# Tokens of v and k by DMA transposes, and the factor of v moved into the decays: a gated linear attention layer on eight cores

## Chip, cores, metric

One Trainium2 chip, eight cores, one program. The metric is the device time of the slowest core, in microseconds (us). Four cores (even numbers) take the first five tiles of a sequence, four (odd numbers) the last three after they have rebuilt the state of the first five.

## What is computed

x has shape (4, 4096, 1024). Cut to what matters here:

```python
h = layernorm(x)
q, k, v = split(silu(causal_conv4(h @ W_qkv.T)))      # 16 heads of 64
z = h @ W_z.T; beta = sigmoid(h @ W_b.T)
g = -exp(A_log) * softplus(h @ W_a.T + dt_bias)
q = l2norm(q) * 64**-0.5; k = l2norm(k)
S_t = S_{t-1} * exp(g_t) + k_t (v_t * beta_t)^T;  o_t = q_t S_t
x = x + (rmsnorm(o) * silu(z)) @ W_out.T
x = x + complex_linear(layernorm(x))                  # 1024 x 1024 in all
```

## The kernel before

The state is advanced in chunks of 128 tokens, four to a tile of 512. With A the running sum of g inside a chunk, a chunk's output is v times the masked product exp(A_t - A_s) (k_s . q_t), plus the old state read by q exp(A_t), and the state is multiplied by the chunk's whole decay and gets k exp(A_end - A_s) times v. beta and the norm of k are factors for each token and head. Before the change their product (beta over the norm) multiplies v, so it is in both uses of v.

Channels lie on partitions after projection and convolution (tile `post`). The two products that sum over tokens need v and k with tokens on partitions. `tvk(g)` does that: 16 transposes of 128x128 on TensorE (8 for v, L731; 8 for k, L735) into the two banks of `pA`, and two multiplications on VectorE that read `pA` and write `vtok` (L741, factor of v) and `ktil` (L746, factor of k). The factors come from `gates_a` to `gates_e`, once for a tile.

The work is software pipelined by hand. The main loop has a tile index t, running one behind the streamed tile u = t + 1, and a step s for each chunk. A step projects and convolves part of tile u, advances the chunk g = 4t + s, finishes the output projection of chunk n - 1 and the last linear layer of chunk n - 2. Each engine runs its instructions in the order in which the loop writes them. `fe` are projections (`proj`, L504, evacuated at L528 on ScalarE and L531 on VectorE), `fc` convolutions (L551) with SiLU (L557), `fz` projections of z. Odd cores run tiles 0 to 4 without outputs (four projections and four convolutions to a step, "state only" steps) and tiles 5 to 7 in full ("full" steps); even cores run five tiles in full. The last tile's four chunks run after the stream has ended, in a loop of their own (the drain).

SyncE (SP) issues nearly all DMAs from one ordered queue: the weights (`w_issue`, five buffers), the convolution's diagonals (`d_issue`, six buffers), rows of x, the stores, and the DMA transposes of the two layernorms (`lnxT` at L140, called from `ln1_norm`, and `ln2T`, from `ln2_norm`). GpSimd (POOL) issues the small loads and stores, masks the decays (L774), squares q (L809), adds the bias (L967) and decays the state (L859). `decay(n, 0)` uses the PSUM pair `pB`, `decay(n, 1)` the pair `pA`, and waits until `tvk` has been read out of it.

## Time and profile before

| | |
|---|---|
| three runs | 884.14 us median (883.65 to 891.31) |
| the profiled execution | 885.31 us |
| span of its slowest core (core 1) | 883.5 us |
| spans of all cores | 871.5 to 883.5 us |
| TensorE busy (core 1) | 680.0 us, 77% |
| VectorE, ScalarE, GpSimd busy | 447.9, 338.4, 192.5 us |
| DMA | 129.58 MB, mean 147 GB/s |

The span runs from the first to the last instruction of a core. The profiled execution took 1.8 us more than the span of its slowest core, and 1.2 us more than the median. The share of busy time is a mean over stages that have different limits, so it has to be read by stage.

### The profile page before, as it was taken

The page shows a single profiled execution, that of the slowest core. Times are in us where ns is not written, and L with a number is a line of the kernel's source. Part 1 is how long each engine was busy: PE and PEld are TensorE (multiplying, and loading weights), DVE is VectorE, ACT ScalarE, POOL GpSimd, SP SyncE. Part 2 cuts the span into 40 slices and gives each one's busy share as a digit, 9 for nine tenths or more (in the row PEclk, how much of TensorE's full clock was granted, in tenths as well). Part 3 has the DMA queues.
Part 4 walks back from the last instruction along what each step waited for, and adds up shares of the span by engine and source line. Part 5 has one row for each costly group of instructions (what it writes and reads, how often), then busy time and mean ns, then how long its engine had stood idle before and what let it go on. Part 6 is the DMA issues. An engine that isn't in the chain of part 4 may idle for free.

```text
span 883.5 us, 14594 instructions; the slowest of 8 cores (871.5 to 883.5 us)
## 1 busy us (share of the span) xinstructions
PE 680.0 (77%) x4872; PEld 317.5 (36%) x4872; DVE 447.9 (51%) x712; ACT 338.4 (38%) x579; POOL 192.5 (22%) x231
## 2 busy tenths in 40 slices
PE   0675569999996998988729997989799997744563
PEld 0322234444443444444204443434344443322221
DVE  2633436677675565445105457734355653557432
ACT  0143426556654464544204653413444433111100
POOL 2020000000001001012113305233142351644310
PEclk9987979999998899999859998989999998767788
DMA  6699458766669566569675556384563474033321
GB/s 150 153 204 194 131 143 214 191 159 190 156 189 222 162 158 193 154 149 172 147 193 167 157 152 164 96 167 118 148 182 93 135 163 102 26 84 86 84 83 36
DMA packets 109618, 129.58 MB, mean 147 GB/s; under 512 B 51990, under 2 KB 72732, under 8 KB 109408
## 3 DMA queue, kind: packets, MB, share of 16 engines
q1 hardware_dynamic: 98832, 106.73, 44.2%
q0 software_dynamic: 10704, 21.83, 14.0%
q8 instruction: 43, 0.70, 0.3%
q14 instruction: 39, 0.32, 0.1%
HBM read 111.39 MB, written 18.27 MB: 147 GB/s over the span
## 4 chain that ended last, share of the span: by engine, by line
PE 47%; DMA 17%; DVE 11%; issue 11%; ACT 9%; SPq 3%; POOL 2%; DVEq 1%; ACTq 0%; POOLq 0%
PE pRG L504 24%; PE pRG L551 6%; DMA dscr<-s_d 5%; PE pRG L934 3%; DMA s_rb<-rscr 3%; ACT s_post L557 3%; PE pB L934 3%; PE pA L976 3%; DMA s_lnxT<-s_lnx 2%; SPq L135 2%; DMA wscr<-s_w 2%; ACT L557 2%; PE pA L731 1%; DMA s_w<-wcat 1%; DMA rscr<-s_r 1%
## 5 line engine op out<-in xcount | busy, mean ns | idle before, releaser
L504 PE MATMUL pRG<-s_lnxT,s_w 128*128 128x512 bf16 x1408 | 341.3, 396 | 51.2 <-DVE s_pre L531 23.6
L504 PEld LDWEIGHTS pRG<-s_lnxT,s_w 128*128 128x128 bf16 x1408 | 136.6, 101 | 221.5 <-issue 82.8
L551 PE MATMUL pRG<-s_pre,s_d 128*128 128x512 bf16 x608 | 149.0, 385 | 10.5 <-ACT s_post L557 7.1
L557 ACT ACTIVATE s_post<-pRG 128x512 bf16<-128x512 f32 x152 | 86.0, 592 | 32.4 <-PE pRG L551 32.1
L528 ACT CAST s_pre<-pRG 128x512 bf16<-128x512 f32 x70 | 41.1, 587 | 142.0 <-PE pRG L504 142.0
L551 PEld LDWEIGHTS pRG<-s_pre,s_d 128*128 128x128 bf16 x608 | 55.3, 98 | 84.4 <-issue 24.8
L859 POOL TENSOR_TENSOR s_S<-s_S,s_gam 128x512 f32<-128x512 f32 x32 | 33.9, 1058 | 234.6 <-DVE s_S L887 219.2
L531 DVE CAST s_pre<-pRG 128x512 bf16<-128x512 f32 x82 | 56.2, 689 | 51.3 <-PE pRG L504 51.2
L415 ACT ACT_TABLE_LOAD x32 | 41.1, 1283 | 78.7 <-DVE s_pre L481 54.5
L557 ACT ACT_TABLE_LOAD x32 | 41.1, 1283 | 37.3 <-PE pRG L551 37.2
L135 POOL DMA_DIRECT2D s_w<-wcat x31 | 16.8, 546 | 140.4 <-DMA wscr<-s_w 64.3
L887 DVE TENSOR_TENSOR s_S<-s_S,pA 128x512 f32<-128x512 f32 x28 | 19.2, 685 | 51.1 <-PE pA L870 45.2
L601 DVE TENSOR_SCALAR s_gt<-s_gt,s_prow 128x128 f32<-128x128 f32 x8 | 2.3, 286 | 81.1 <-ACT s_gt L599 81.1
L574 ACT ACTIVATE s_zT<-pRG 128x512 bf16<-128x512 f32 x24 | 14.1, 597 | 75.1 <-PE pRG L504 64.2
L564 ACT ACTIVATE s_ksq<-s_post 128x512 bf16<-128x512 bf16 x64 | 40.3, 630 | 5.9
L741 DVE TENSOR_TENSOR s_vtok<-pA,s_ekT 128x1024 bf16<-128x1024 bf16 x30 | 36.6, 1220 | 1.4 <-PE pA L731 1.0
L746 DVE TENSOR_TENSOR s_ktil<-pA,s_ekT 128x1024 bf16<-128x1024 bf16 x30 | 36.5, 1216 | 0.0
L135 POOL DMA_DIRECT2D rscr<-s_r x24 | 13.8, 579 | 101.8 <-ACT s_r L905 40.2
L387 DVE TENSOR_TENSOR s_d<-s_i128f,s_cw 128x512 bf16<-128x512 f32 x24 | 16.4, 722 | 38.3 <-DMA dscr<-s_d 33.7
L967 POOL TENSOR_TENSOR s_x<-s_x,s_biasb 128x1024 f32<-128x1024 f32 x12 | 25.5, 2125 | 43.3 <-DVE s_ln L957 43.3
L976 PE MATMUL pA<-s_wbig,s_ln2T 128*128 128x512 bf16 x112 | 27.3, 400 | 8.1 <-DMA s_ln2T<-s_ln 8.1
L774 POOL TENSOR_SCALAR_AFFINE_SELECT s_dsb<-s_dsb 128x1024 bf16<-128x1024 bf16 x20 | 22.9, 1143 | 22.9 <-ACT s_dsb L770 22.8
(161 smaller groups left out, 821.4 us busy)
## 6 DMA issues: line engine op xcount, KB each, us to landing
s_w<-wscr SPq DMA_DIRECT2D x144, 256.0 KB, 3.5
s_d<-dscr SPq DMA_DIRECT2D x128, 128.0 KB, 4.0
s_xa<-x SPq DMA_DIRECT2D x30, 512.0 KB, 5.2
s_w<-wcat POOLq DMA_DIRECT2D x32, 256.0 KB, 6.4
wscr<-s_w SPq DMA_DIRECT2D x32, 256.0 KB, 5.1
s_x<-x SPq DMA_DIRECT2D x14, 512.0 KB, 5.4
s_rb<-rscr POOLq DMA_DIRECT2D x24, 256.0 KB, 5.3
y<-s_x SPq DMA_DIRECT2D x12, 512.0 KB, 2.9
```

Source lines behind the costliest of these rows:

```text
L135: lane.e.dma_start(out=out, in_=in_).then_inc(self.h, 16)
L415: t = S.mark(S.e.activation(out=bn[:, 14:15], in_=bn[:, 13:14], func=AF.Ln, bias=EPS5))
L504: ins = P.e.matmul(ps, w[:, dc * 128:(dc + 1) * 128], lnxT[u % 2][:, dc, :], start=(dc == 0), stop=(dc == 7))
L528: te = S.mark(S.e.copy(out=pre[:, j, 3:515], in_=ps))
L531: te = V.mark(V.e.tensor_copy(out=pre[:, j, 3:515], in_=ps))
L551: ins = P.e.matmul(ps, dr[i % ND][:, tap * 128:(tap + 1) * 128], pre[:, j, tap:tap + 512], start=(tap == 0), stop=(tap == 3))
L557: silu_tok[(u, cc)] = ring_free[k] = S.mark(S.e.activation(out=post[u % 2][:, cc, :], in_=ps, func=AF.Silu))
L564: ksq_tok[(u, cc)] = S.mark(S.e.activation(out=ksq[kb], in_=post[u % 2][:, cc, :], func=AF.Square))
L741: tv[g] = V.mark(V.e.tensor_tensor(out=buf("v", n).rearrange("p (h w) -> p h w", w=64), in0=pAb[:, 0:1024].rearrange("p (h w) -> p h w", w ...
L746: tk[g] = V.mark(V.e.tensor_tensor(out=buf("k", n).rearrange("p (h w) -> p h w", w=64), in0=pAb[:, 1024:2048].rearrange("p (h w) -> p h w" ...
L934: ins = P.e.matmul(ps[:, hf * 512:(hf + 1) * 512], buf("ga", n)[:, cc * 128:(cc + 1) * 128], wout[:, cc, hf * 512:(hf + 1) * 512], start=( ...
L976: ins = P.e.matmul(ps[:, hf * 512:(hf + 1) * 512], ln2T[n % 2][:, dg, :], wbig[:, dg, hf * 512:(hf + 1) * 512], start=(dg == 0), stop=(dg ...
```

## The change

1. `tvk` is two DMA transposes on SP, `post` to `vtok` and `post` to `ktil`, in four new DMA slots. It is called for chunk g + 1 late in the step of chunk g (behind the convolutions and, in full steps, behind `outproj` and `ln2_stats`, before `ffn`); SP waits there for the SiLUs of v and k and for the matmuls of `state(g)`, which read `vtok` and `ktil`. In the drain it stands behind `state_decay`.
2. `post` is laid out by chunk, 24 x 128 columns each, so that the eight blocks of v or of k of one chunk are contiguous. SiLU writes and Square reads four pieces of 128 columns.
3. v keeps no factor. A new `kscale(g)` multiplies `ktil` in place on VectorE by one factor for each token and head. It stands behind `ln1_norm` in the step, in the drain behind `oT`.
4. The factor of v goes into the exponents. The log of beta over the norm is subtracted from A on the side of the source token. `gates_a` computes the a and b parts in separate columns of PSUM with 16-column weights (64 matmuls of 128 columns for a tile in place of 32), `gates_b` has one Exp more and its Ln is 256 columns wide, `gates_c` has one addition in place of one of a single column, and the three-part bf16 split `a3` is 256 wide and moves from `gates_b` (step s = 0) to `gates_c` (s = 2), as does its store. `gates_b3`, three loads on POOL, moves from s = 0 to s = 3.
5. `decay(n, 1)` no longer waits for `ktil`, as `tvk` is out of `pA`.
6. `r32` shares the buffer of `ssb`; the wait for the store of `r32` moves from ScalarE (`r_act`) to the copy into `ssb` on VectorE.

```diff
-            P.need(*psA_free[0])
-            P.need(t_i128b, silu_tok[(t, 23)], silu_tok[(t, 15)])
-            for j in range(8):
-                ins = P.e.transpose(out=pAb[:, j * 128:(j + 1) * 128],
-                                    in_=po[:, 16 + j, c * 128:(c + 1) * 128], identity=i128b)
...
-            V.need(t1_, ek_tok[t], old(Uo_tok, n))
-            tv[g] = V.mark(V.e.tensor_tensor(
...
-            tk[g] = V.mark(V.e.tensor_tensor(
...
-            psA_free[0] = [tk[g]]
+            free = stream_done[NT - 2] if n == N0 else Uo_tok.get(n - 1 if n < N0 else n - 2)
+            Y.need(silu_tok[(t, 23)], silu_tok[(t, 15)], free)
+            tv[g] = q_tv[g % 2].gotr(Y, buf("v", n).rearrange("p (a b) -> p a b", a=8),
+                                     post[t % 2][:, c, 16 * 128:24 * 128])
+            tkr[g] = q_tk[g % 2].gotr(Y, buf("k", n).rearrange("p (a b) -> p a b", a=8),
+                                      post[t % 2][:, c, 8 * 128:16 * 128])
+
+        def kscale(g):
+            t, c = g // 4, g % 4
+            kk = buf("k", g - 4 * NPRE).rearrange("p (h w) -> p h w", w=64)
+            V.need(tkr[g], ek_tok[t])
+            tk[g] = V.mark(V.e.tensor_tensor(
+                out=kk, in0=kk,
+                in1=ekT[t % 2][:, 16 * c:16 * c + 16, None].broadcast_to([128, 16, 64]),
+                op=ALU.mult))
...
+            for ab in range(2):
+                for dc in range(8):
+                    for c in range(4):
+                        ins = P.e.matmul(pG[32 * c:32 * c + 16, 128 * ab:128 * ab + 128],
+                                         wab[:, dc, 16 * ab:16 * ab + 16],
+                                         lnxT[u % 2][:, dc, c * 128:(c + 1) * 128],
+                                         start=(dc == 0), stop=(dc == 7), tile_position=(0, 32 * c))
...
         def gates_c(u):
+            S.need(k2_tok[(u, 15)], A_tok[u])
+            t = S.mark(S.e.activation(out=gx[:, 0:128], in_=pG[:, 256:384], func=AF.Ln, bias=EPS6))
+            V.need(t, A_tok[u])
+            t = V.mark(V.e.scalar_tensor_tensor(out=gx[:, 0:128], in0=gx[:, 0:128], scalar=0.5,
+                                                op0=ALU.mult, in1=gx[:, 128:256], op1=ALU.add))
+            V.need(t)
+            t = gtok["At"] = V.mark(V.e.tensor_tensor(out=gA[:, 128:256], in0=gA[:, 0:128],
+                                                      in1=gx[:, 0:128], op=ALU.add))
...
                 ln1_norm(m)
+                if att:
+                    kscale(g)
...
-                if streaming and s == 0:
+                if streaming and s == 3:
                     gates_b3(u)
...
                 fc(8)
+                if att or (t == -1 and s == 3):
+                    tvk(g + 1)
                 fz(2)
```

## Rows read from the trace of the kernel before

**Rows 1.** Cores: span and mean granted clock, the slowest odd and even.
```profile
core 1: 883.5 us, clock 0.913
core 6: 883.2 us, clock 0.921
```

**Rows 2.** Windows, core 1: stretch, length, busy PE/PEld/DVE/ACT/POOL, clock, DMA share, GB/s.
```profile
133.80:344.90 211.10, 189.94 (x1465) 92.69 (x1464) 136.49 (x249) 119.83 (x199) 16.37 (x17) 0.98 0.71 184
344.90:506.00 161.10, 130.27 (x886) 59.27 (x885) 64.87 (x112) 64.47 (x108) 35.00 (x50) 0.92 0.66 162
506.00:718.50 212.50, 190.89 (x1410) 88.89 (x1408) 117.98 (x156) 87.02 (x149) 71.59 (x80) 0.96 0.55 144
718.50:883.50 165.00, 96.97 (x712) 44.64 (x706) 73.06 (x83) 25.50 (x48) 53.79 (x55) 0.79 0.29 74
```

**Rows 3.** Windows of core 6, its full steps in the stream.
```profile
188.20:715.00 526.80, 469.62 (x3457) 221.30 (x3517) 310.51 (x404) 220.82 (x384) 179.15 (x203) 0.97 0.57 155
```

**Rows 4.** Chain that ended last, core 1, a state-only step: start, length, what.
```profile
215.83 0.45 PE pA L731 x8
216.28 0.45 PE pA L735 x8
...
223.68 3.11 DMA s_lnxT<-s_lnx
```

**Rows 5.** Groups, core 1, 121 to 345 us: busy, mean ns, idle before.
```profile
L731 PE MATMUL pA<-s_i128b,s_post 128*128 128x128 bf16 x128 | 9.8, 219 | 0.0
L735 PE MATMUL pA<-s_i128b,s_post 128*128 128x128 bf16 x128 | 9.8, 219 | 0.0
L432 DVE TENSOR_SCALAR s_lnx<-s_xa,s_bnA 128x1024 bf16<-128x1024 f32 x16 | 13.0, 811 | 0.0
```

**Rows 6.** Groups of instructions, core 1, whole span.
```profile
L588 PE MATMUL pRG<-s_lnxT,s_wab 128*32 128x128 bf16 x256 | 6.3, 254 | 24.8 <-DMA s_lnxT<-s_lnx 23.8 <-DVE s_lnxT L444 1.1
L746 DVE TENSOR_TENSOR s_ktil<-pA,s_ekT 128x1024 bf16<-128x1024 bf16 x30 | 36.5, 1216 | 0.0
```

**Rows 7.** Waits of PE, core 1, 506 to 718.5 us: total, times, longest.
```profile
PE pRG L504 <- DVE s_pre L531: 6.2, 3, 5.0
PE pRG L504 <- DMA s_w<-wscr: 3.5, 1, 3.5
PE pA L764 <- DVE s_ktil L746: 2.2, 2, 1.8
```

**Rows 8.** Waits of PE, core 6, 188 to 715 us.
```profile
PE pRG L504 <- DMA s_w<-wscr: 19.3, 6, 4.0
...
PE pRG L504 <- DVE s_pre L531: 7.8, 9, 1.2
...
PE pA L764 <- DVE s_ktil L746: 4.8, 6, 1.8
```

**Rows 9.** Groups of instructions, core 6, 188 to 715 us.
```profile
L432 DVE TENSOR_SCALAR s_lnx<-s_xa,s_bnA 128x1024 bf16<-128x1024 f32 x11 | 34.0, 3087 | 0.0
```

**Rows 10.** Tile s_lnxT on SP, core 1, 121 to 345 us: ns min/median/max; landing.
```profile
L140 SPq DMA_TRANSPOSE s_lnxT<-s_lnx x16: 1217/1218/5641, 131.2 to 340.2; - x16
...
DMA to landing us min/median/max: 3.1/3.1/10.4
```

**Rows 11.** Windows, core 1, around one DMA transpose that runs alone.
```profile
869.50:871.50 2.00, 0.00 (x0) 0.00 (x0) 0.00 (x0) 0.00 (x0) 1.19 (x1) 0.50 0.68 131
```

**Rows 12.** Timeline of SP and PE, core 1, end of a state-only step.
```profile
225.60 1.81 SPq L135 DMA_DIRECT2D s_d<-dscr  x4
...
225.84 0.44 PE L870 MATMUL pA<-s_vtok,s_ktil 128*64 128x64 bf16 x16
```

**Rows 13.** The chain that ended last, core 1: the first operation of the split.
```profile
349.00 0.24 DVE s_a L610
```

**Rows 14.** Timeline and windows of core 1 in the drain.
```profile
777.77 1.08 POOL L135 DMA_DIRECT2D s_rb<-rscr  x2
...
784.13 3.54 DVE L918 TENSOR_TENSOR s_w<-s_w,s_rb 128x1024 bf16<-128x1024 bf16 x1 [3.22 <-DMA s_rb<-rscr]
...
779.00:781.00 2.00, 0.00 (x0) 0.00 (x0) 1.36 (x3) 0.00 (x0) 1.01 (x2) 0.79 1.01 311
```

More of the change, by code:

```diff
@@ L193, in build_program @@
     lhalo = sb("s_lhalo", [128, 8, 4])
-    post = [sb(f"s_post{i}", [128, 24, TT]) for i in range(2)]
+    post = [sb(f"s_post{i}", [128, NCH, 24 * 128]) for i in range(2)]
     zT = sb("s_zT", [128, 8, TT])
@@ L557, in conv @@
             silu_tok[(u, cc)] = ring_free[k] = S.mark(S.e.activation(
-                out=post[u % 2][:, cc, :], in_=ps, func=AF.Silu))
+                out=post[u % 2][:, :, cc * 128:cc * 128 + 128],
+                in_=ps.rearrange("p (a b) -> p a b", a=4), func=AF.Silu))
             k2_flush(2)
@@ L564, in conv @@
                 ksq_tok[(u, cc)] = S.mark(S.e.activation(
-                    out=ksq[kb], in_=post[u % 2][:, cc, :], func=AF.Square))
+                    out=ksq[kb].rearrange("p (a b) -> p a b", a=4),
+                    in_=post[u % 2][:, :, cc * 128:cc * 128 + 128], func=AF.Square))
                 pend_k2.append((u, cc, kb))
@@ L579, in emit @@
         A_tok = {}
[L580 removed]
+        gate_free = [t_mem]
         sA = {}
@@ L585, in gates_a @@
             P.need(t_wab, gate_free[0])
-            for dc in range(8):
-                for c in range(4):
-                    ins = P.e.matmul(pG[32 * c:32 * c + 32, 0:128], wab[:, dc, :],
-                                     lnxT[u % 2][:, dc, c * 128:(c + 1) * 128],
-                                     start=(dc == 0), stop=(dc == 7), tile_position=(0, 32 * c))
+            for ab in range(2):
[5 more added lines that the diff above has]
+                                         start=(dc == 0), stop=(dc == 7), tile_position=(0, 32 * c))
@@ L591, in gates_a @@
             gtok["ab"] = P.mark(ins)
         def gates_b(u):
-            S.need(gtok["ab"], t_prow, gtok.get("At"))
-            t = S.mark(S.e.activation(out=ga, in_=pG[:, 0:128], func=AF.Exp,
-                                      scale=prow[:, 0:1], bias=prow[:, 1:2]))
+            S.need(gtok["ab"], t_prow, gtok.get("tr"), gtok.get("a3"))
+            S.e.activation(out=gx[:, 0:128], in_=pG[:, 0:128], func=AF.Exp, bias=prow[:, 0:1])
+            t = S.mark(S.e.activation(out=gx[:, 128:256], in_=pG[:, 128:256], func=AF.Exp,
+                                      scale=-1.0))
@@ L733, in tvk @@
-            t1_ = P.mark(ins)
-            for j in range(8):
-                ins = P.e.transpose(out=pAb[:, 1024 + j * 128:1024 + (j + 1) * 128],
-                                    in_=po[:, 8 + j, c * 128:(c + 1) * 128], identity=i128b)
-            t2_ = P.mark(ins)
-            e = ekT[t % 2]
-            n = g - 4 * NPRE
-            V.need(t1_, ek_tok[t], old(Uo_tok, n))
-            tv[g] = V.mark(V.e.tensor_tensor(
-                out=buf("v", n).rearrange("p (h w) -> p h w", w=64),
-                in0=pAb[:, 0:1024].rearrange("p (h w) -> p h w", w=64),
-                in1=e[:, 32 * c + 16:32 * c + 32, None].broadcast_to([128, 16, 64]), op=ALU.mult))
@@ L1054, in emit @@
         S.need(t_prow)
-        t = S.mark(S.e.activation(out=prow[:, 7:8], in_=prow[:, 2:3], func=AF.Exp))
+        t = S.mark(S.e.activation(out=prow[:, 3:4], in_=prow[:, 1:2], func=AF.Exp))
         V.need(t)
-        t_coef = V.mark(V.e.tensor_scalar(out=prow[:, 6:7], in0=prow[:, 7:8], scalar1=-1.0,
+        t_coef = V.mark(V.e.tensor_scalar(out=prow[:, 2:3], in0=prow[:, 3:4], scalar1=-1.0,
                                           scalar2=None, op0=ALU.mult))
@@ L1130, in emit @@
                     gates_c(u)
-                if att:
-                    tvk(g)
                 if on2:
@@ L1215, in emit @@
             if n == N0:
-                tvk(g)
+                kscale(g)
                 r_load(n - 1)
@@ L1228, in emit @@
             state_decay(g)
+            if more:
+                tvk(g + 1)
             xr_load(n)
@@ L1231, in emit @@
             if more:
-                tvk(g + 1)
+                kscale(g + 1)
             state(g, "D")
```

128 lines of the change are left out of this document (56 added, 72 removed).

## The prediction

> **What bounds the kernel now.** I read the spans of the cores first, because two kinds of core run different work. The slowest of each kind are level [rows 1], so the change must help both. Next I cut each core into its stages. Core 1 keeps TensorE busy for 189.9 of 211.1 us in its state-only steps and for 190.9 of 212.5 us in its full steps, with the clock granted at 0.96 to 0.98. In between, while weights of q and z are used for the first time, PE has 31 us idle in 161; in the drain it is busy for 97 of 165 [rows 2]. Core 6 is busy for 469.6 of 526.8 us in its full steps [rows 3]. So the streamed stages are bound by PE and the rest by chains of waits. Then I read the chain that ended last: in a state-only step the transposes of `tvk` lie on it (0.45 + 0.45 us), and at a tile's end so does the landing of the last `lnxT` transpose [rows 4]. Last I read the groups of one stretch, for the prices, and PE's waits, for what the removed VectorE work holds up.
>
> **The change, part by part,** on core 1, against its span of 883.5 us.
>
> *PE loses the transposes.* 256 of them were busy for 9.8 + 9.8 us over 16 steps [rows 5], 1.22 us a step. They are on PE's path there: 16 steps give -19.6 us.
>
> *DMA gets two transposes a step.* One alone fills 0.68 of the 16 engines over 2 us [rows 11], 1.36 us of all of them. A state-only step is 211.1/16 = 13.2 us and uses 0.71 of it, 9.4 us [rows 2]. With 2.7 more it needs 12.1 us, just what PE then needs (211.1 - 19.6 = 191.5, 12.0 a step). Two resources that close delay each other; I take 12.3 us a step, which gives back 5 us. The ends are 0 (weights are loaded five ahead, and loads in flight may overlap better than the share says) and 19.6 (all of it).
>
> *SP gets two issues of 1.22 us* [rows 10]. They are behind the diagonals' loads and the state's matmuls [rows 12], ahead of the next weights' loads. Those serve a projection of the next step, so in the stream 2.4 us of SP are covered. In 344.9 to 506 us, where the kernel waits for first stores and loads that SP issues in order, they aren't. There are five chunks: I take half of the PE saving (-3.0) and two chunks that pay 2.4 us (+4.9), so +2; ends -6 and +12.
>
> *Landing of v and k.* The existing transposes of this shape land in 3.1 us [rows 10]. The state's matmuls start at 225.84, SP is free of the diagonals at 227.41 [rows 12], so the second transpose is issued at about 228.7 and is there by 232. `kscale` needs it about 10 us after the state's matmuls: at 236 or so. Nothing waits. The Trainium skill, "VectorE: DVE Perf Modes", section "The three transpose paths", has 1309 ns for a 128x128 block by DMA and 390 ns on TensorE, and its rules say to use TensorE where PSUM will do. By its figure eight blocks are 10.5 us; the row has 3.1 for eight, so I don't take it.
>
> *VectorE loses two multiplications that read PSUM, 1.22 us each* [rows 6], and gets `kscale`, of the same width from SBUF. I take 1.22 us for it, and as its upper end the 3.54 us that the one multiplication of that shape with both inputs in SBUF took beside POOL's work [rows 14]. In state-only steps POOL is hardly busy (16.4 us of 211 [rows 2]), and all projections are evacuated before `kscale`, so nothing of PE's stands behind it. In full steps the evacuations of the fifth and seventh projection do. But `ln2_norm` and `ln1_norm` now come 2.4 us earlier on VectorE, ahead of POOL's busy time, and so do the weights' loads behind them on SP. `lnx` takes 3.09 us on core 6's full steps and 0.81 in the state-only steps of core 1 [rows 5, 9]: most of that is waiting, and it should shrink. The wait of `decay(n, 1)` for `ktil` goes: -2.2 us [rows 7]. Of PE's waits for evacuations and weights, 6.2 + 3.5 us [rows 7], I take half, -4.9; ends 0 and -9.7. The PE saving of the eight chunks from 506 to 718.5 is 8 x 1.22 = -9.8. For SP and DMA there I give back 0.2 us a chunk, +1.6.
>
> *Gates.* 32 matmuls for a tile cost 6.3/8 = 0.79 us [rows 6]. They become 64 of half the width in weights and the same in columns: eight tiles give +6.3 us. The lower end is 0, if the narrow ones run denser. The extra Exp and the wider Ln (some 0.6 us of ScalarE) stand beside the next projection. The split has five operations on VectorE, the first of them 0.24 us at half the new width [rows 13], so at most 5 x 0.5 with the waits between; it moves to s = 2, where it takes the place of the two multiplications. Its store and the three loads on POOL have a step or more until `decay` needs them. I cost these at nothing; without that cover it is 1.5 us for each of three tiles.
>
> *Drain.* The chain goes through POOL's load of `rb` (issued 777.8), the gate multiplication (784.13, 3.54 us) and the projection [rows 14]. `vtok` and `ktil` are not on it, so nothing is gained. The new transposes are issued just before that load, into DMA engines that are full from 779 to 781 [rows 14]: up to 2.7 us for three chunks, +8. `kscale`, ahead of the state's sum, waits for them and pushes POOL's squares behind the multiplication that they slow now: up to -1.3 us each, -4. I take 0.
>
> Sum for core 1: -19.6 + 5 + 2 - 9.8 - 2.2 - 4.9 + 1.6 + 6.3 = -21.6, a span of 861.9. The execution took 1.8 us more than the span, and 1.2 more than the median: 862.5.
>
> Core 6 has 16 chunks in the stream: -19.5; -4.8 and half of 19.3 + 7.8 from its waits [rows 8]; gates +4, DMA and SP +3. That is -31, so it ends ahead and core 1 sets the time.
>
> **Rivals.**
>
> *Slower: the transposes land late and close a loop.* `vtok` and `ktil` have one buffer, so SP may issue the next pair only when the state's matmuls are done, and these wait for `kscale`, which waits for the landing. The loop is about 1.6 us until SP is free, 1.22 for v, the landing, 1.22 for `kscale`, 0.44 for the matmuls. It decides from a landing of 8 us on. Against it stands the median of 3.1 us; for it the longest, 10.4 [rows 10], under a large load, and the engines' share, which rises from 0.71 to above 0.9. With 10.4 us a step is 14.9 us: 16 steps cost +27 in place of -14.6, and the sum is 904. This is also what the 10.5 us of the Trainium skill, worked out above, would do.
>
> *Unchanged or little faster: DMA takes the whole gain.* State-only steps stay at 13.2 us because the engines' 12.1 us can't be packed closer. Core 1 then loses 14.6 us of gain: 877. For it: the share is already 0.71 as a mean. Against it: weights are five loads ahead, and PE waited there for no weight.
>
> *The new multiplication is blocked by POOL.* In full steps `kscale` takes 3.54 us like the row of the drain, 2.3 more, eight times, and the evacuations behind it wait: +18 at most, half of it likely, 871 to 881. Here the Trainium skill speaks against the change: "SBUF — State Buffer", section "Who interferes with whom", says that a VectorE instruction with two SBUF inputs and a GpSimd one that reads SBUF exclude each other for the whole instruction, and one with a single SBUF input is free. By it the removed pair was free and the new one isn't. Rows 14 and rows 9 agree in kind; whether it reaches PE is the question.
>
> *More: all waits go.* The bank, the evacuations and the weights no longer hold PE, gates cost nothing, DMA packs: 862.5 - 5 - 4.9 - 6.3 = 846.
>
> **How the numbers follow.** Forecast 862.5 (855 to 870) 0.50, blocked multiplication 0.13, DMA takes the gain 0.14, more 0.10, slower 0.13. The range of 8 in 10 takes in all but most of the slower case and the far end of the best: 849 to 884. 1% is 8.8 us, about what a measurement of this kernel can tell from no change; 875.3 and 893 are the bounds. Faster has the forecast, the best case, most of the blocked multiplication and a part of the third: 0.72. Same has the rest of these two and the mild end of the loop: 0.17. Slower 0.11.
>
> **What would show it.** In the profile after, the state-only steps of core 1 should be about 12.3 us apart by the state decays on POOL, with a DMA share near 0.95; the new transposes should land in 3 to 6 us, and `kscale` should have hardly any idle time before it. In full steps `lnx` should be well under 3 us on core 6, and PE should wait less for weights. In the drain the `rb` load should stay near 6 us. The prediction is wrong if VectorE is idle for the new transposes, if PE waits for `ktil` ahead of the state's matmuls, or if SP's issues grow beyond 1.22 us.

## Result and profile after

The changed kernel took 902.5 us (median of 4 runs, 896.63 to 903.64) against 886.0 us (883.65 to 891.31) of the kernel before on the same chip: ratio 1.0164, 95% interval [1.0097, 1.0231]. It is slower by 1.6%, and outside the predicted range of 849 to 884 us. The profiled execution took 901.92 us.

The spans of the cores after, against [rows 1]:

```profile
core 0: 899.8 us, clock 0.895
core 1: 899.3 us, clock 0.882
...
core 3: 867.7 us, clock 0.905
...
core 5: 864.7 us, clock 0.907
core 6: 896.7 us, clock 0.889
core 7: 899.8 us, clock 0.882
```

Of the odd cores, which do the same work, 3 and 5 are 32 to 35 us ahead of 1 and 7. Before, 3 was at 879.0 and 5 at 881.5 us. So part of the change's effect hits some cores and spares others, and it is large. Of the even cores, 0 and 6 end 13 to 17 us behind 2 and 4.

Windows of core 1 after, cut at the state decays on POOL, which mark the chunks (columns as in [rows 2]): ten state-only steps, two steps in which something stands still, the heart of that stall (not cut at decays), seven full steps.

```profile
136.90:264.30 127.40, 117.78 (x872) 52.86 (x871) 82.15 (x160) 79.62 (x135) 10.42 (x10) 1.00 1.01 238
264.30:326.40 62.10, 24.90 (x197) 11.73 (x196) 16.19 (x31) 14.54 (x25) 2.63 (x4) 0.70 1.02 125
285.00:311.00 26.00, 0.64 (x16) 0.54 (x16) 2.60 (x4) 0.00 (x0) 0.52 (x1) 0.50 1.08 86
505.60:732.60 227.00, 208.64 (x1549) 95.07 (x1546) 131.28 (x174) 103.06 (x177) 82.16 (x92) 0.97 0.71 173
```

The first two stages on core 3, cut at its own decays:

```profile
133.60:266.70 133.10, 120.85 (x874) 54.31 (x873) 82.76 (x160) 79.73 (x135) 10.43 (x11) 0.98 1.00 227
266.70:301.90 35.20, 24.46 (x197) 11.63 (x195) 16.04 (x31) 14.54 (x25) 2.63 (x4) 0.85 1.01 217
```

The two steps take 62.1 us on core 1 and 35.2 on core 3, with the same work in them (PE busy 24.9 and 24.5). Before they took 35.3 us on both. In the 26 us of the stall PE does 0.64 us of work and is granted 0.50 (1.2 GHz), and the DMA engines are busy for 1.08 of their time, yet move only 86 GB/s; in the ten steps ahead it was 238.

The chain that ended last on core 1 leads through this place:

```profile
268.98 7.19 SPq L131
...
276.26 8.73 SPq L131
...
285.11 25.81 DMA s_lnxT<-s_lnx
310.92 0.14 issue
311.06 1.88 PE pRG L590 x48
```

SyncE needs 7.2 and 8.7 us to issue one load of weights, and a transpose of the layernorm lands after 25.8 us, where the median before was 3.1 [rows 10]. The timeline of SyncE and GpSimd on core 1 shows what came just before:

```profile
263.75 1.28 SPq L136 DMA_TRANSPOSE s_vtok<-s_post  x1
265.07 2.58 SPq L136 DMA_TRANSPOSE s_ktil<-s_post  x1
...
265.31 0.59 POOL L131 DMA_DIRECT2D s_wout<-woutd  x1
...
267.75 17.24 SPq L131 DMA_DIRECT2D s_w<-wscr  x4
285.11 21.15 SPq L136 DMA_TRANSPOSE s_lnxT<-s_lnx  x1
```

`wout`, 2 MB of weights of the output projection, is one load of GpSimd in both kernels and the largest of all transfers (the next ones have 512 KB). It now meets the transposes of v and k. Its landing and that of `s_ktil` in the view of the DMAs (last column: us from issue to landing), core 1 after:

```profile
s_wout<-woutd POOLq DMA_DIRECT2D x1, 2048.0 KB, 41.5
...
s_ktil<-s_post SPq DMA_TRANSPOSE x1, 42.3
```

and core 1 before:

```profile
s_wout<-woutd POOLq DMA_DIRECT2D x1, 2048.0 KB, 15.3
```

Over the cores 0 to 7 this landing was 20.2, 15.3, 20.2, 15.4, 20.6, 16.1, 21.5 and 15.3 us before; after it is 38.1, 41.5, 21.7, 14.5, 22.0, 15.4, 38.8 and 47.8. The four cores where it took 1.8 to 3.1 times as long, 0, 1, 6 and 7, are the four that end last.

On even cores the load stands ahead of the first chunk, so its price shows there: the first state decay of cores 0 and 6 came at 204.4 and 207.7 us (188.9 and 188.2 before), that of cores 2 and 4 at 192.6 and 194.8 (188.3 and 183.8).

In a small form the meeting was there before. On core 1 of the kernel before, a transpose of the layernorm was issued at 277.25 us, beside `wout`; SyncE took 5.64 us to issue it, it landed after 10.4, and PE waited 7.9 us for it. The same two steps take 26.2 us when the load is cut up (e12 below), 9 less than the 35.3. The longest issue and the longest landing in [rows 10] are this event.

That isn't all. Core 6 in its full steps, against [rows 3] (522.0 us here, 526.8 there):

```profile
205.00:727.00 522.00, 465.99 (x3387) 212.05 (x3387) 310.59 (x394) 221.07 (x390) 188.05 (x201) 0.96 0.69 175
```

From its first to its last state decay in the stream core 6 took 518.9 us (core 0 525.5, core 2 524.4, core 4 521.7; this stretch is called its stream below); before these were 526.7, 524.5, 522.4 and 521.3. The forecast had 31 us less. Its groups of instructions on VectorE, the answer to [rows 9]:

```profile
L746 DVE TENSOR_TENSOR s_ktil<-s_ktil,s_ekT 128x1024 bf16<-128x1024 bf16 x15 | 46.7, 3112 | 0.0
...
L429 DVE TENSOR_SCALAR s_lnx<-s_xa,s_bnA 128x1024 bf16<-128x1024 f32 x11 | 14.7, 1336 | 0.0
L955 DVE TENSOR_SCALAR s_ln<-s_x,s_bnB 128x1024 bf16<-128x1024 f32 x14 | 11.4, 811 | 10.2 <-ACT s_bnB L414 10.2
```

The multiplication of k has a mean of 3112 ns, where it took 1215 before. `lnx` fell from 3087 to 1336, and `ln`, the second normalisation, from 1315 to 811; that they shrink was forecast; but VectorE's sum stayed at 310.6 us (310.5 before). PE's waits on core 6, the answer to [rows 8]:

```profile
PE pB L825 <- DVE s_dsb L793: 24.2, 9, 7.8
PE pRG L548 <- DVE s_pre L528: 11.3, 5, 3.1
PE pRG L501 <- DVE s_pre L528: 6.1, 3, 2.5
PE pRG L501 <- DMA s_w<-wscr: 4.9, 5, 1.6
```

The wait for weights fell from 19.3 to 4.9 us, and the one for `ktil` is gone. In their place PE waits for the masked products (L793; 10.9 us before) and for evacuations ahead of the convolution (0.3 before). One of these, in the timeline of core 6:

```profile
443.65 1.55 POOL L773 TENSOR_SCALAR_AFFINE_SELECT s_dsb<-s_dsb 128x1024 bf16<-128x1024 bf16 x1
444.18 4.20 DVE L746 TENSOR_TENSOR s_ktil<-s_ktil,s_ekT 128x1024 bf16<-128x1024 bf16 x1
...
445.18 2.11 POOL L965 TENSOR_TENSOR s_x<-s_x,s_biasb 128x1024 f32<-128x1024 f32 x1
...
447.26 2.01 POOL L857 TENSOR_TENSOR s_S<-s_S,s_gam 128x512 f32<-128x512 f32 x1
448.30 1.21 DVE L793 TENSOR_TENSOR s_dsb<-pB,s_dsb 128x1024 bf16<-128x1024 f32 x1
...
449.96 0.64 PE L825 MATMUL pB<-s_dsb,s_vtok 128*64 128x128 bf16 x8 [6.88 <-DVE s_dsb L793]
```

The multiplication runs for 4.20 us while three operations of GpSimd run, the masked products stand behind it, and PE is idle for 6.88 us.

Both of its operands are in SBUF now. Before, one came out of PSUM, and then GpSimd did not lengthen it. Core 6 before:

```profile
319.81 1.11 POOL L774 TENSOR_SCALAR_AFFINE_SELECT s_dsb<-s_dsb 128x1024 bf16<-128x1024 bf16 x1
320.31 1.22 DVE L746 TENSOR_TENSOR s_ktil<-pA,s_ekT 128x1024 bf16<-128x1024 bf16 x1
320.87 1.90 POOL L809 TENSOR_TENSOR s_qsq<-s_post 128x1024 bf16<-128x1024 bf16 x1
```

GpSimd works through the whole of it, and it takes 1.22 us, like all 15 of them in the stream.

### The profile page after: what moved, and what is told of

Its sections match the earlier page's. It is cut to its first block, busy times and chain, and to the rows that moved or that the text cites. A ratio compares the mean times of both kernels' runs of the same rounds, so it can differ in the third digit from the quotient of the medians.

```text
span 899.8 us, 14152 instructions; the slowest of 8 cores (864.7 to 899.8 us)
## 1 busy us (share of the span) xinstructions
PE 656.8 (73%) x4616; PEld 293.5 (33%) x4616; DVE 414.7 (46%) x681; ACT 338.2 (38%) x587; POOL 195.4 (22%) x231
## 4 chain that ended last, share of the span: by engine, by line
PE 43%; DMA 23%; DVE 9%; issue 9%; ACT 7%; SPq 7%; POOL 1%; DVEq 0%; ACTq 0%; POOLq 0%
PE pRG L501 22%; DMA dscr<-s_d 6%; PE pRG L548 6%; DMA s_lnxT<-s_lnx 5%; DMA wscr<-s_w 5%; SPq L131 4%; PE pRG L932 3%; PE pA L974 3%; SPq L136 3%; PE pB L932 3%; ACT s_post L554 2%; ACT L554 1%; DMA s_rb<-rscr 1%; DMA s_ktil<-s_post 1%; PE pRG L974 1%
## 5 line engine op out<-in xcount | busy, mean ns | idle before, releaser
L548 PE MATMUL pRG<-s_pre,s_d 128*128 128x512 bf16 x608 | 147.8, 382 | 8.6 <-ACT s_post L554 6.8
L548 PEld LDWEIGHTS pRG<-s_pre,s_d 128*128 128x128 bf16 x608 | 55.4, 98 | 81.4 <-issue 21.3
L746 DVE TENSOR_TENSOR s_ktil<-s_ktil,s_ekT 128x1024 bf16<-128x1024 bf16 x30 | 46.1, 1536 | 51.0 <-DMA s_ktil<-s_post 51.0
L868 PE MATMUL pA<-s_vtok,s_ktil 128*64 128x64 bf16 x448 | 12.7, 201 | 40.3 <-DVE s_ktil L746 40.3
L605 DVE TENSOR_SCALAR s_gx<-s_gx,s_prow 128x128 f32<-128x128 f32 x8 | 2.3, 286 | 85.4 <-ACT s_gx L603 85.4
L885 DVE TENSOR_TENSOR s_S<-s_S,pA 128x512 f32<-128x512 f32 x28 | 19.2, 684 | 36.6 <-PE pA L868 33.6
L131 POOL DMA_DIRECT2D rscr<-s_ssb x24 | 13.9, 580 | 99.9 <-ACT s_ssb L903 37.5
```

Source lines behind the costliest of these rows:

```text
L131: lane.e.dma_start(out=out, in_=in_).then_inc(self.h, 16)
L548: ins = P.e.matmul(ps, dr[i % ND][:, tap * 128:(tap + 1) * 128], pre[:, j, tap:tap + 512], start=(tap == 0), stop=(tap == 3))
L746: tk[g] = V.mark(V.e.tensor_tensor(out=kk, in0=kk, in1=ekT[t % 2][:, 16 * c:16 * c + 16, None].broadcast_to([128, 16, 64]), op=ALU.mult))
```

## Experiments

Two causes were to be told apart: the meeting of `wout` with the transposes, and VectorE's new multiplication. Rivals to both were the transposes themselves, in every step, and the wider gates. The ratio is always to the kernel before on the same chip. That kernel took 888.0 us on the chip of e1 to e4, 892.4 on that of e5 to e8, 888.9 for e9 to e11, 887.6 for e12 and e13, 888.9 for e14 and e15. So between these groups the ratios compare better than the times.

**e1: the changed kernel again.** No edit.

> The changed kernel as it is, as a yardstick on this chip. Both theories: 897 to 904 us. The theory of the collision (the 2 MB load of wout and the new transposes of v and k, in flight together, bring the DMA engines nearly to a halt) expects that some cores again show a landing of wout near 40 us and others near 15 to 22 us, and that the core that sets the time is one of the first kind. The rival (the loss is spread: the new multiplication that POOL holds up in full steps, and a longer queue on SP where stores and first loads are awaited) expects the landing of wout to have no bearing on which core is last.

906.8 us, ratio 1.0223 [1.0165, 1.0281]. The loss is there again, a little above what both theories had. In the profiled execution `wout` landed after 21.7, 25.4, 37.8, 28.1, 22.5, 49.3, 36.1 and 36.5 us on cores 0 to 7. The longest, 49.3, is that of core 5, which ended last (903.7 us) and had been spared in the first profile; its two steps took 69.1 us. That is what the theory of the collision said, and it isn't a matter of which core. Later runs on this chip are compared with this one.

The two profiles together point at what decides. `wout` landed after more than 25 us on the ten cores where GpSimd issued it 0.24 to 3.93 us after SyncE had begun to issue the transpose of k of the same step. On the six others, with 14.5 to 22.5 us, it was issued at most 0.12 us or at least 4.06 us after. So it seems to be the timing of the two issues that decides, not the core. The margins are thin, 0.12 and 0.13 us, and this was read from two profiles after the fact; no run moved the load by some microseconds.

**e2: the changed kernel without the load of `wout`** (set to zero once, so the output projection gives zero).

```
-                if t == max(NPRE - 3, -1) and s == 3:
-                    late["wout"] = cload(G, wout.rearrange("p a b -> p (a b)"), d_wout)
+                late["wout"] = None
```

> The changed kernel without the load of wout (it is filled with zeros at the start, so the output projection adds nothing). Theory of the collision: the slowest core loses the stall of 18 to 25 us, 880 to 884 us, and the spread of the cores of one kind falls from 35 us to below 10. Rival: 895 us or more, for the load itself is only 7 us of the 16 DMA engines, and the kernel before shows that it can be hidden.

887.6 us, ratio 1.0008 [0.9972, 1.0045]. The two steps of the stall take 25 us on core 1 (272 to 297). The time is 4 to 8 us above what the theory had, far from its rival's 895: the odd cores end at 862 us, and the even cores, at 877 to 890, set the time.

**e3: the kernel before without that load.** The same edit.

> The kernel before without the load of wout (zeros in its place). It is the price of the load where nothing collides with it: the trace of before has one stall of about 9 us beside it on odd cores and a few us on even cores. Both theories: 874 to 882 us. If it falls by 15 us or more, the stall of the changed kernel is nothing new and the theory of the collision falls.

883.0 us, ratio 0.9928 [0.9897, 0.9959]. The load costs 5.0 us before (888.0 to 883.0) and 19.2 after (906.8 to 887.6). So the meeting is worth 14 us of the change's loss. But without any load of `wout` the change is still no gain: 887.6 against 883.0, where the forecast had 21.6 us of gain.

**e4: `wout` in eight loads** of 256 KB, one in each of eight steps (even cores two in each of the four steps ahead of the stream).

```
+                if NPRE == 0 and t == -1:
+                    wout_part(2 * s, 2)
+                if NPRE > 0 and t in (NPRE - 3, NPRE - 2):
+                    wout_part(4 * (t - NPRE + 3) + s, 1)
```

> The changed kernel with the load of wout cut into eight of 256 KB: two in each of the four steps before the first chunk on even cores, one in each of eight steps on odd cores. All work is done. Theory of the collision: it needs the large load beside the transposes, so 881 to 887 us, nearly what leaving the load out gives. Rival: 897 to 904 us, unchanged.

892.8 us, ratio 1.0058 [1.0028, 1.0088]: 14.0 us back, with the whole load in place (6 us above the theory's range). A piece lands in 7.1 us on core 1 (the view of the DMAs), and the stalled steps take 25.1 us:

```profile
s_wout<-woutd POOLq DMA_DIRECT2D x3, 256.0 KB, 7.1
```

This settles the first cause. e4 is the base of most of what follows.

**e5: the multiplication of k earlier** (e4's base), at the place where `tvk` multiplied before, ahead of the step's normalisations.

```
+                if att:
+                    kscale(g)
                 if on1:
                     r_load(n1)
...
-                if att:
-                    kscale(g)
```

> The changed kernel with the load of wout in eight pieces (892.8 us) and the new multiplication of k moved to where the two of before stood: behind the first evacuation of a step, ahead of ln2_norm. Theory of the shared work with POOL: there POOL is idle, so the multiplication takes 1.2 us in place of 3.1, PE waits for the masked products (24 us on an even core) fall by half, and the full steps of an even core fall from 520 to 529 us to about 508: 876 to 883 us. Rival (full steps are held by DMA and SP, whose share rose from 0.57 to 0.69): the time stays within 4 us of 892.8, though the multiplication gets shorter.

933.9 us, ratio 1.0489 [1.0397, 1.058]; the gain that the theory expected did not come. On the even cores the multiplication fell to 1218 ns, but `lnx` and `ln` rose to 2.0 and 1.66 us (core 6) and the stream was no shorter (526.7 to 531.1 us). The odd cores, at 925 to 934 us, set the time (861 to 872 in e4): there the multiplication comes before the landing of k, VectorE's evacuations stand behind it, and a state-only step of core 1 takes 15.2 us. VectorE's and PE's waits of core 1 from 147 to 372 us:

```profile
DVE s_ktil L746 <- DMA s_ktil<-s_post: 56.7, 14, 8.3
...
PE pRG L548 <- DVE s_pre L528: 36.8, 12, 6.6
```

Two things follow. In both orders it is the operation with its operands in SBUF beside GpSimd's that gets longer, so order alone moved the loss from one to another. And the first rival of the prediction, a landing that is waited for, is real as soon as the multiplication stands early.

**e6: no DMA transposes at all** (e4's base; `vtok` and `ktil` are set to zero once and only the multiplication of k is done).

```
-            tv[g] = q_tv[g % 2].gotr(Y, buf("v", n).rearrange("p (a b) -> p a b", a=8),
-                                     post[t % 2][:, c, 16 * 128:24 * 128])
-            tkr[g] = q_tk[g % 2].gotr(Y, ...)
+            tv[g] = silu_tok[(t, 23)]
+            tkr[g] = free
```

> The same base without the two DMA transposes of each chunk: v and k in token order stay zero, so the attention's output and state are zero. All else is issued, the multiplication of k too. It prices the transposes (SP issues, DMA engines, landing) with wout no longer in their way. Theory of the shared work with POOL: little changes on even cores, 886 to 893 us, for the multiplication still stands in POOL's busy time. Rival: 872 to 880 us.

880.2 us, ratio 0.9889 [0.981, 0.9969]. That is the rival's time nearly, though the theory was right on the streams. The odd cores' spans fell to 845.1 to 849.1 us (861.3 to 872.3 in e4); the even cores' streams stayed at 519 to 526 us. The even cores, which set the time, gained ahead of their first state decay (183.7 to 187.6 us, 187.7 to 195.3 in e4) and a little in the drain (164 to 168 us, 166 to 169). Windows of core 1, state-only steps:

```profile
135.60:263.70 128.10, 117.46 (x870) 52.77 (x869) 81.58 (x160) 81.11 (x138) 12.02 (x13) 1.00 0.76 198
```

So in the even cores' full steps the transfers cost next to nothing, and what eats the gain there is elsewhere. And even with no transfer and no transpose a state-only step is 12.8 us, not the 12.0 that the forecast's subtraction had.

**e7: the gates' part alone**: the factor of v in the exponents as changed, v and k turned on TensorE, v copied out of PSUM (683 ns), k multiplied out of PSUM, at the old places, `wout` in one load.

```
+            for j in range(8):
+                ins = P.e.transpose(out=pAb[:, j * 128:(j + 1) * 128],
+                                    in_=po[:, c, (16 + j) * 128:(17 + j) * 128], identity=i128b)
...
+            tv[g] = V.mark(V.e.tensor_copy(out=buf("v", n), in_=pAb[:, 0:1024]))
```

> One part of the change alone: the factor of v in the exponents (wider gates, later split and store, later loads of b3) and the chunked layout, but v and k turned on TensorE into PSUM, v copied out by VectorE without a factor, k multiplied out of PSUM, at the old places; wout loaded at once, as before. It prices the new gates. I expect +2 to +8 us to before, 890 to 896: 64 narrow matmuls for a tile where 32 stood (6 us on odd cores, 4 on even) and the split in the stretch where first stores are awaited. If it is level with before, the whole loss lies in the DMA transposes and the new multiplication.

888.9 us, ratio 0.9968 [0.9938, 0.9997]. The wider gates, the later split included, cost nothing that can be measured, and 0.54 us less of VectorE a chunk brings little.

**e8: the split's store later on GpSimd** (e4's base), out of the way of the loads ahead of it.

```
-            G.need(t)
-            sA["st"] = q_a.go(G, ascr[u - NPRE]...., a3)
...
+                G.need(gtok["a3"])
+                sA["st"] = q_a.go(G, ascr[u - NPRE]...., a3)
```

> The base (892.8 us) with the store of the split issued by POOL behind the step's weight loads and the stores of the decays, not ahead of them. In the changed kernel POOL waits for the split at the start of step s = 2, and where weights are still loaded by POOL their loads queue behind that wait. Theory that this order costs part of the time before the first chunk (even) and from 364 to 506 us (odd): 3 to 6 us less, 887 to 890. Rival: nothing, as in those stretches the stores of the diagonals set the pace.

896.5 us, ratio 1.0018 [0.9966, 1.0071], not distinguishable from e4's. The split's store isn't where the time went.

**e9: without the multiplication of k** (e4's base; VectorE still waits for the landing, k goes unscaled into the state).

```
-            tk[g] = V.mark(V.e.tensor_tensor(
-                out=kk, in0=kk,
-                in1=ekT[t % 2][:, 16 * c:16 * c + 16, None].broadcast_to([128, 16, 64]),
-                op=ALU.mult))
+            tk[g] = tkr[g]
```

> The changed kernel with wout loaded in 8 pieces, as in e4_after_wout8, and without the multiplication of k on VectorE: VectorE still waits for the transposed k to land, but k goes unscaled into the state update, so the output is not the reference's. Theory (the multiplication, 3.1 us in a full step beside GpSimd's masked products where the forecast had 1.22, delays VectorE's other work and with it TensorE): the even cores' stream falls from 520 to 529 us to about 505 to 510, and TensorE's waits for the masked products and the convolution's evacuations shrink; ratio near 0.99. Rival (VectorE's time in a full step is not what sets its length; something else, such as the waits for weights or TensorE's own rows, is late next): even cores stay at 519 to 526 us and only the odd ones lose some 10 us.

864.4 us, ratio 0.9729 [0.9686, 0.9773]: 28 us less than e4, on another chip. The even cores' streams are 497.9 to 504.5 us (520.4 to 529.0 in e4). The window of core 6:

```profile
205.00:727.00 522.00, 473.53 (x3425) 215.76 (x3424) 269.78 (x386) 223.73 (x396) 188.71 (x211) 0.98 0.73 175
```

VectorE has 40.8 us less than after (in the same window, though the stream of e9 ends 30 us earlier). Of PE's waits for the masked products 11.9 us are left (20.5 in e4), and those ahead of the convolution are gone. So VectorE's work ahead of the masked products sets the length of the even cores' full steps, and the multiplication is the part of it that grew. But this run leaves it out altogether, where a kernel that is right needs 1.22 us for it even when nothing lengthens it; so the 28 us are more than what its lengthening costs.

**e10: v by DMA, k on TensorE** (e4's base): eight transposes into one bank of `pA`, multiplied on the way out. Transposes and multiplication stand at the old place, ahead of the normalisations, so the run changes two things at once.

```
+            for j in range(8):
+                ins = P.e.transpose(out=pAb[:, 1024 + j * 128:1024 + (j + 1) * 128],
+                                    in_=post[t % 2][:, c, (8 + j) * 128:(9 + j) * 128],
+                                    identity=i128b)
...
-                out=kk, in0=kk,
+                out=buf("k", n).rearrange("p (h w) -> p h w", w=64),
+                in0=pAb[:, 1024:2048].rearrange("p (h w) -> p h w", w=64),
```

> The changed kernel with wout in 8 pieces, v by DMA transpose as changed, and k turned by 8 TensorE transposes into PSUM and multiplied on its way out by VectorE, so that the multiplication reads one operand from SBUF, at about 0.8 to 1.2 us. Theory (of k the multiplication in place is what costs, of v the DMA transpose is a gain): 870 to 882 us, ratio 0.98 to 0.995, the multiplication near 1.2 us on the even cores. Rival (the full steps are bound elsewhere): odd cores 860 to 870 us, even cores as in e4, 880 to 893 us, ratio 1.00 within 0.005.

878.4 us, ratio 0.9894 [0.9861, 0.9927]. Core 6, groups of instructions:

```profile
L429 DVE TENSOR_SCALAR s_lnx<-s_xa,s_bnA 128x1024 bf16<-128x1024 f32 x11 | 29.2, 2650 | 0.0
L961 DVE TENSOR_SCALAR s_ln<-s_x,s_bnB 128x1024 bf16<-128x1024 f32 x14 | 23.2, 1654 | 4.6 <-ACT s_bnB L414 4.6
...
L750 DVE TENSOR_TENSOR s_ktil<-pA,s_ekT 128x1024 bf16<-128x1024 bf16 x14 | 17.0, 1216 | 0.1
```

The multiplication is back at 1216 ns, and the two normalisations are back at their long times. The streams of the even cores, 516.7 to 527.0 us, are hardly shorter than in e4 (520.4 to 529.0); most of the gain over e4 lies ahead of their first state decay (182.6 to 186.8 us, 187.7 to 195.3 in e4).

**e11: e10 with `wout` in one load.**

> As e10_w8_kpe, with wout loaded at once as in both given kernels. Theory (the 2 MB load and the DMA transposes slow each other, in proportion to how many transposes meet it): half of the added transposes leave about half of the 14 us that the split load gave back, 6 to 8 us over e10_w8_kpe. Rival (a single transpose in front of the queue is enough to hold SyncE until the load has passed): the full 14 us. Wout's landing on the cores shows which: 15 to 20 us as before, or 38 to 48 us as with the change.

889.5 us, ratio 1.001 [0.998, 1.004]: 11 us over e10, between what the two expected. But `wout` lands in 15.4 us on core 1, as in the kernel before, so the long stall is gone with one transpose a chunk:

```profile
s_wout<-woutd POOLq DMA_DIRECT2D x1, 2048.0 KB, 15.4
```

The two steps take 35.6 us on core 1 as before, and 25.6 with the load in pieces. The 10 us between are the short stall of the kernel before: SyncE takes 7.14 us to issue the layernorm's transpose, and PE waits 9.3 us for it. With two transposes a chunk the load cost 37 us on core 1. The even cores, which set the time in both runs, end at 881.1 to 886.3 us (870.2 to 876.5 in e10): their first state decay is at 188.4 to 189.9 us (182.6 to 186.8), and their streams take 524.6 to 533.2 us (516.7 to 527.0).

**e12: the kernel before with `wout` in eight loads.** The edit of e4.

> The kernel before with wout loaded in 8 pieces, nothing else changed: what the split load is worth by itself. Theory (in the kernel before the load cost about 5 us in all, by e3_before_nowout, since no transposes met it): 3 to 6 us less than before, ratio 0.993 to 0.997, so that of the gain of e10_w8_kpe about half is the transposed v. Rival (the whole gain of e10_w8_kpe is the split load): ratio 0.99, 878 to 881 us.

884.2 us, ratio 0.9958 [0.9934, 0.9982]. The split load by itself is worth 3.4 us. So e10, with ratio 0.9894, has 0.6% from the rest of the change, v's transposes and the factor in the exponents; the intervals just don't touch.

**e13: e10 with the normalisations of the full steps on ScalarE.**

```
+            t = S.mark(S.e.activation(out=bn[:, 16:17], in_=bn[:, 15:16], func=AF.Copy, scale=-1.0))
+            t = S.mark(S.e.activation(out=bn[:, 17:18], in_=bn[:, 12:13], func=AF.Identity,
+                                      scale=bn[:, 16:17]))
+            return S.mark(S.e.activation(out=out, in_=in_, func=AF.Identity,
+                                         scale=bn[:, 15:16], bias=bn[:, 17:18]))
```

> e10_w8_kpe with both layer normalisations of the full steps (29.2 and 23.2 us of VectorE on core 6 in 522 us) moved to ScalarE, which is busy 209 of these 522 us: two small operations and one of 128x1024 each. Theory (VectorE's time sets the length of a full step while TensorE has work ready, as e9_w8_nokscale showed with 28 us for 49 us taken away): even cores' stream from 517 to 527 us to 500 to 510, ratio 0.965 to 0.98. Rival (the normalisations hold nothing up, only the multiplication of k stood in front of the masked products; and ScalarE's own chain of exponentials is delayed by them): no change or slower, ratio 0.99 to 1.01.

859.5 us, ratio 0.9686 [0.9651, 0.972], 19 us less than e10. The window and a group of core 6, and then the window of e10:

```profile
205.00:727.00 522.00, 469.52 (x3423) 218.87 (x3479) 260.38 (x367) 254.68 (x454) 181.44 (x207) 0.96 0.67 166
...
L426 ACT ACTIVATE s_lnx<-s_xa,s_bnA 128x1024 bf16<-128x1024 f32 x11 | 13.6, 1240 | 1.0
```

```profile
205.00:727.00 522.00, 472.68 (x3413) 215.85 (x3412) 301.68 (x387) 209.26 (x370) 183.51 (x204) 0.96 0.63 163
```

VectorE gives up 41 us, ScalarE takes 45, at 1.24 us a normalisation where VectorE had 1.65 to 2.65.

**e14: both v and k by DMA with the same relief** (e4 with e13's edit).

> The changed kernel with wout in 8 pieces (e4_after_wout8) and the normalisations of the full steps on ScalarE as in e13_w8_kpe_lna; both v and k by DMA transpose. Theory (the multiplication of k takes 3.1 to 3.3 us of VectorE a chunk where e13_w8_kpe_lna has 1.2, so 32 us more of VectorE in the full steps, of which half to two thirds showed in e9_w8_nokscale): 15 us or so slower than e13_w8_kpe_lna, 868 to 880 us, ratio 0.975 to 0.99. Rival (with room on VectorE the multiplication is hidden and TensorE's 8 transposes fewer a chunk come through): as fast as e13_w8_kpe_lna or faster, 850 to 862 us, ratio 0.955 to 0.97.

879.0 us, ratio 0.9864 [0.98, 0.9928], as the theory said. Core 6, groups:

```profile
L761 DVE TENSOR_TENSOR s_ktil<-s_ktil,s_ekT 128x1024 bf16<-128x1024 bf16 x15 | 32.4, 2162 | 0.0
```

**e15: the kernel before with the same two edits**: `wout` in pieces, normalisations on ScalarE, v and k on TensorE.

> The kernel before with wout in 8 pieces and the normalisations of the full steps on ScalarE; v and k on TensorE. Theory (VectorE late in the kernel before too, by less, so part of the relief comes through; then TensorE's transposes bind): 865 to 875 us, ratio 0.975 to 0.985, slower than e13_w8_kpe_lna by 6 to 12 us. Rival (the whole gain of e13_w8_kpe_lna is the move of the normalisations and owes nothing to the change): 856 to 863 us, ratio 0.965 to 0.972.

860.0 us, ratio 0.9665 [0.962, 0.9709]: the rival was right. Window of core 6:

```profile
205.00:727.00 522.00, 480.33 (x3568) 225.92 (x3567) 270.01 (x383) 257.98 (x455) 187.10 (x209) 0.97 0.58 157
```

It and e13 are the fastest versions, not to be told apart. With VectorE relieved, v by DMA in place of TensorE is worth nothing that can be measured, and v and k by DMA lose 2% (e14 against e15).

## Why the prediction was wrong

The sign was wrong. Two steps failed: "SP gets two issues of 1.22 us", which left out what the new transposes would meet, and "I take 1.22 us for `kscale`", with the relief of VectorE that was built on it. One by one:

- **"PE loses the transposes", 19.6 us on PE's path in state-only steps.** Mis-sized. The 1.22 us a step were busy time, not time on the path: e6, with neither transposes nor transfers, has 12.8 us a step against 13.5 before, 0.67 less. PE's busy time fell by 8.1 us in ten steps (125.57 in the kernel before, 117.46 in e6), with about 1.5 of gates added, and its idle time rose by 1.4. The count was off too: 133.8 to 344.9 us hold the transposes of 15 chunks, not 16, 344.9 to 506 six, not five, and 506 to 718.5 six, not eight; a state-only step took 13.5 us between decays, not 13.2. That is worth some 3 us of the sum.
- **"DMA gets two transposes a step", 12.3 us a step.** Cores 3 and 5 took 13.3 us a step, cores 1 and 7 12.7 and 12.9, all at 13.5 before, with the DMA share at 1.00 and 1.01 on cores 3 and 1. Against the 12.8 to 12.9 of e6 the transfers cost from nothing to 0.5 us a step, 0.2 in the mean, where 0.3 was taken. The rival "DMA takes the whole gain" came near on cores 3 and 5, where 0.2 us a step is left, and not on the other two.
- **"SP gets two issues of 1.22 us", +2 (-6 to +12).** This is the step that failed for the stall, for what it left out. In the stages that it speaks of it held within its ends: from the step after the stall to chunk 20 the odd cores took 173.6 to 179.2 us after and 169.0 to 175.4 before, some 4 us more, and 166.8 to 171.2 in e6. But it took the duration of an issue as fixed, and did not ask which other load the new transposes would meet. GpSimd's 2 MB load of `wout` was in the trace, the largest of all transfers, and the longest issue and landing of [rows 10], 5.6 and 10.4 us, were its work on a transpose that was there already. It meets them at 265 us, SyncE's issues grow to 21 us, and core 1 loses 27 us in two steps. e2, e3 and e4 show it: 14 us of the median, of which 3.4 come back in the kernel before too (e12). The prediction's own rival for a late landing named "a large load", and priced it as 10.4 us in every step, where it is one event, a landing of 25.8 us.
- **"Landing of v and k: nothing waits."** Right outside the stall. From 133 to 264 us the transposes of k landed in 3.3 to 7.7 us, median 4.5. e5 shows how narrow it was: with the multiplication earlier VectorE waits 14 times for them, and a state-only step takes 15.2 us. That is near the rival's 14.9, but by luck: the rival had it from a landing of 10.4 us and a closed loop, and in e5 k lands after 5.9 us in the median on core 1, and PE waits for evacuations that stand behind the waiting multiplication. The Trainium skill ("VectorE: DVE Perf Modes", "The three transpose paths") has 1309 ns a block; the estimate of 10.5 us for eight, worked out from it, isn't borne out by the median of 4.5. The advice of the same page of the Trainium skill ("Rules for kernel authors") to use TensorE where PSUM will do is what e15 against e14 came to.
- **"I take 1.22 us for `kscale`".** This is the step that failed for the even cores: 3.11 us on core 6 after, 2.58 in core 1's full steps. The upper end that the prediction itself gave, 3.54, was the nearer. Leaving the multiplication out gives back 28 us (e9). The same product took 1.22 us with one operand in PSUM, also where GpSimd worked beside it. These numbers agree with the rule of the Trainium skill, "SBUF — State Buffer", section "Who interferes with whom", on two SBUF inputs. The Trainium skill frees a single SBUF input there only outside the modes that use two ports, which the prediction left out, and it names `tensor_scalar` as an operation that can enter them; the rows agree there too, as `lnx`, a `tensor_scalar` with one such input, took 811 to 3087 ns. The prediction priced this rival at eight chunks of core 1. It is sixteen on the even cores, where of the forecast 31 us core 6 kept 7.8 in its stream and the others nothing. Its size alone isn't the whole of it: where the multiplication took 1.22 us again (e5, e10), the streams were no or hardly shorter.
- **"`lnx` should shrink", and the relief of PE's waits.** Right in its mechanism: 3087 to 1336 ns, waits for weights 19.3 to 4.9 us on core 6. But VectorE's sum didn't change (310.5 and 310.6 us), because other short and long operations that read and write SBUF grew: against 26.3 us less of normalisations and 18.3 less of `vtok` stand 28.5 more for the multiplication of k, 4.9 for the copies of `s_halo`, 4.6 for `s_rhs`, 2.7 for `s_eb`, and 3.3 for the gates with the split at its new width. PE's waits moved to L825 and L548. The time lost beside GpSimd did not go away with one victim; it went to the next.
- **"Core 6 ends ahead and core 1 sets the time."** Wrong. Once the stall was gone (e2, e4) the even cores set the time. They are bound by VectorE's part in a full step as much as by PE. This lay in the first step: PE busy for 469.6 of 526.8 us was read as bound by PE, while giving two normalisations of VectorE to ScalarE takes off 19 us (e10 to e13) and 24 (e12 to e15) with PE's work as it was.
- **Full steps of core 1, -15.3 for eight chunks.** Near: seven steps took 227.0 us, 239.2 before, -12.2.
- **Gates, +6.3.** They measured +4.7 us of PE busy time (6.3 to 11.0 over eight tiles), and e7, which has the gates and the split as changed, shows no cost in time.

```profile
L590 PE MATMUL pRG<-s_lnxT,s_wab 128*16 128x128 bf16 x512 | 11.0, 254 | 18.2 <-DMA s_lnxT<-s_lnx 17.2 <-DVE s_lnxT L441 1.0
```

(That is the group of core 1 after, the answer to [rows 6].)

- **Drain, 0.** From the last streamed chunk to the end the even cores took 167 to 170 us, 163.6 to 168 before: some 2 us more, within its ends.

What stays open: why the even cores' streams are longer in e11 than in e10, long after the load has landed; and why the load and the transposes slow each other at all, and why only when the load is issued 0.24 to 3.93 us after the transpose of k, if that holds beyond two profiles. That they do is shown by leaving out and by cutting up the load, not by a view into the queues. Not tested is the remedy that comes to mind first for the second cause, less work of GpSimd at that place in place of less of VectorE.

## What to carry to other kernels

Before a transfer is added to each step, list the large transfers that it can meet once, on any queue, and cut the large one into pieces: here that gave back 14 of the 19 us that the change cost on that chip. Look for it in the rows of the kernel before: the longest issue and landing of a group, against its median, showed the same meeting in a small form. An engine that is busy for 59% of a stage can still set its length, when its long instructions stand ahead of what the busiest engine waits for; a run in which some of its work is left out, or moved to another engine, shows it. A multiplication that has to be done anyway is cheap on the way out of PSUM; with both operands in SBUF and beside GpSimd it took 2.6 times as long.

## What the runs showed of the hardware

- A 2 MB load of GpSimd and DMA transposes of 128x1024 on SyncE slow each other: landings of 41.5 and 42.3 us where 15.3 and 3.1 were usual, engines at a share of 1.08 moving 86 GB/s. It happened on the ten cores of two profiles where the load was issued 0.24 to 3.93 us after the issue of the transpose of k had begun, and on none of the six others. With one transpose a chunk (e11) the load landed in 15.4 us on core 1.
- The issue of a DMA is not of fixed length: a transpose took 1.22 us, 5.64 beside `wout` in the kernel before, 1.86 in the median under the load of the state-only steps after, and 21.15 in the stall. The view of SyncE's transposes of k on core 1, 133 to 264 us:

```profile
L136 SPq DMA_TRANSPOSE s_ktil<-s_post x10: 1342/1864/4196, 139.9 to 252.2; - x10
...
DMA to landing us min/median/max: 3.3/4.5/7.7
```

- The multiplication of 128x1024 with both operands in SBUF took 3112 ns beside GpSimd's work and 1218 with both in SBUF at a time when GpSimd did little (e5, core 6). With one operand in PSUM it took 1215, also with GpSimd at work for its whole length (core 6 before).
- A normalisation of 128x1024 from f32 took 1240 ns on ScalarE each time, and 811 to 3087 on VectorE, by what GpSimd did beside it.
